# Asking for room in a ring of 24 once for six gathers

## What is computed

```python
h_self = x @ W_self.T + b_self
messages = x[src] @ W_neigh.T + b_neigh
h_neigh = jax.ops.segment_sum(messages, dst, num_segments=x.shape[0])
h = jax.nn.relu(h_self + h_neigh)
y = x + h
out = (y - mean(y)) / sqrt(var(y) + 1e-5)      # over the 128 features
```

## Time and profile before

| | before |
|---|---|
| median of three runs | 691.28 us (684.82 to 696.59) |
| the profiled execution | 693.77 us, span of its instructions 692.0 us |
| TensorE busy | 531.8 us (77%) |
| VectorE busy | 423.4 us (61%) |
| GpSimd busy | 405.3 us (59%), 391 gathers among it |
| ScalarE busy | 352.0 us (51%) |
| mean granted clock of TensorE | 0.88 of 2.4 GHz |

### The profile page before, as it was taken

How to read it: one execution, slowest core, us unless ns; L and a number is a source line. 1 busy time by engine, 2 the same in 40 slices (tenths; PEclk the granted TensorE clock), 3 DMA queues, 4 the chain that set the end, 5 groups by cost and what they waited for, 6 DMA issues and landing times.

```text
span 692.0 us, 12704 instructions
## 1 busy us (share of the span) xinstructions
PE 531.8 (77%) x3281; PEld 468.0 (68%) x3281; DVE 423.4 (61%) x1919; ACT 352.0 (51%) x1049; POOL 405.3 (59%) x424
## 2 busy tenths in 40 slices
PE   2046187878899769778877988888987897789895
PEld 0035076767778758667766867777877787678794
DVE  7883267688867657867747664644554535555564
ACT  1010055456555454655654655565655556456686
POOL 4777566666666645766557656656556656565400
PEclk9999589899798878988989989997789799888998
DMA  2422134444444454454443544444444434444443
GB/s 78 123 59 56 53 89 134 113 122 136 126 121 133 132 151 118 123 135 128 128 121 103 162 126 125 129 129 123 120 121 131 128 110 133 134 134 128 126 127 85
DMA packets 122942, 82.20 MB, mean 119 GB/s; under 512 B 15374, under 2 KB 115894, under 8 KB 122840
## 3 DMA queue, kind: packets, MB, share of 16 engines
q1 hardware_dynamic: 109208, 53.63, 27.5%
q0 software_dynamic: 13664, 27.77, 15.4%
HBM read 55.44 MB, written 26.71 MB: 119 GB/s over the span
## 4 chain that ended last, share of the span: by engine, by line
PE 61%; issue 15%; DVE 9%; another core or an unknown queue 6%; ACT 5%; DMA 2%; ACTq 1%; SPq 1%; POOL 0%; DVEq 0%
PE bank L889 17%; PE bank L912 16%; PE bank L913 13%; PE bank L877 6%; PE bank L908 5%; PE bank L894 3%; ACT result L1023 2%; DVE pick L730 2%; DVE y L740 2%; ACT sums_t L996 2%; DMA x_in<-in_x 1%; DVE below L530 1%; DMA end_dst<-in_dst 1%; ACT std L1013 1%
## 5 line engine op out<-in xcount | busy, mean ns | idle before, releaser
L482 POOL DMA_INDIRECT ring<-in_x,chunk_src x391 | 380.9, 974 | 236.3 <-issue 87.6
L996 ACT COPY sums_t<-bank 128x192 f32 x391 | 124.6, 319 | 290.5 <-remote 109.4
L889 PE MATMUL bank<-pick,ring 128*128 128x193 f32 (+1 forms) x782 | 188.8, 367 | 42.2 <-DVE pick L730 17.4
L912 PE MATMUL bank<-wsum_t,x_t 128*128 128x128 f32 (+1 forms) x782 | 188.3, 328 | 0.0
L913 PE MATMUL bank<-wn_t,sums_t 128*128 128x128 f32 (+1 forms) x782 | 174.5, 310 | 1.0 <-issue 0.9
L889 PEld LDWEIGHTS bank<-pick,ring 128*128 128x128 f32 x782 | 141.3, 215 | 49.5 <-issue 29.0
L1023 ACT ACTIVATE result<-y,minus_mean,rstd 128x128 f32<-128x128 f32 x391 | 163.5, 486 | 0.0
L912 PEld LDWEIGHTS bank<-wsum_t,x_t 128*128 128x128 f32 (+1 forms) x782 | 138.1, 221 | 26.8 <-issue 26.7
L740 DVE SCALAR_TENSOR_TENSOR y<-bank,x_in 128x384 f32<-128x384 f32 x131 | 72.6, 554 | 134.2 <-PE bank L913 65.2
L913 PEld LDWEIGHTS bank<-wn_t,sums_t 128*128 128x128 f32 (+1 forms) x782 | 141.1, 225 | 0.3 <-issue 0.2
L730 DVE TENSOR_SCALAR pick<-columns,local 128x194 f32<-128x194 f32 x391 | 106.3, 328 | 0.2
(11 more groups left out here) (118 smaller groups left out, 195.8 us busy)
## 6 DMA issues: line engine op xcount, KB each, us to landing
x_in<-in_x SPq DMA_DIRECT2D x130, 192.0 KB
out<-result SPq DMA_DIRECT2D x130, 192.0 KB
ring<-in_x,chunk_src POOLq DMA_INDIRECT x391
degrees_t<-degrees_dram SPq DMA_DIRECT2D x130, 2.2 KB
dst_padded<-in_dst SPq DMA_DIRECT2D x1, 390.6 KB
src_padded<-in_src SPq DMA_DIRECT2D x1, 390.6 KB
edge_src<-in_src SPq DMA_DIRECT2D x1, 390.6 KB
edge_dst<-in_dst SPq DMA_DIRECT2D x1, 390.6 KB
```

The lines of the kernel that those rows point to most:

```text
L482: nc.gpsimd.indirect_dma_start(ring[:, c % RING, :], None, x, bass.IndirectOffsetOnAxis(ap=chunk_src[:, c:c + 1], axis=0)).then_inc(gather ...
L889: ins = mm(into[:, frame:frame + SPAN + carried], ring[:, c % RING, :], pick[tau % DEEP][:, c % TRIO, 0:SPAN + carried], start=(c == 0), s ...
L912: mm(h, x_t[b][:, q, 0:rows], k.wsum_t[:], start=False, stop=False)
L996: nc.scalar.copy(sums_t[:, bass.ds(at, SPAN)], sum_bank[c // PAIR % SUM_BANKS][:, frame:frame + SPAN]).then_inc(sums_placed, 1)
```

## The change

GpSimd no longer asks for its place in the ring at every gather. At c = 24, 30, 36, ... it asks once for the six places of c to c + 5, that is, until chunk c + 5 - 24 is summed, and then issues six gathers. The last question, at c = 390, is the same as it was, since only one chunk is left. The question for the trio eight before stays. Everything else stays; all lines behind 76 move by one (L482 becomes L483).

```diff
 RING = 24
+BURST = 6
 GATHER_SEMS = 8
@@
                 if c % TRIO == 0 and tau >= GATHER_SEMS:
                     pool.wait_ge(gathered[tau % GATHER_SEMS], gathers_upto(tau - GATHER_SEMS))
-                if c >= RING:
-                    pool.wait_ge(chunks_summed, c - RING + 1)
+                if c >= RING and c % BURST == 0:
+                    pool.wait_ge(chunks_summed, min(c + BURST, CHUNKS) - RING)
                 nc.gpsimd.indirect_dma_start(ring[:, c % RING, :], None, x,
```

## The result

The changed kernel takes 723.66 us, the median of 5 runs (720.52 to 732.77); the kernel before, run beside it, 686.8 us (5 runs, 684.82 to 696.59). The ratio is 1.051, with an interval of 1.045 to 1.056: **about 5% slower**, where no change was forecast. The ratio leaves out executions in which the core was in a slower state, and the profiled one, the longest of the five with 732.77 us and a span of 731.0, is among these, so its rows overstate the loss by about 9 us.

The account below looks back on a forecast made before the run. TensorE's trios were taken to bound the kernel. Questions removed, the stricter question and other DMA work summed to 0 on TensorE's path: 693.8 us profiled again, median 691.3 us, range for 8 in 10 683 to 700.

Parts of the forecast that it names:

- A gather matters only where TensorE waits for its rows: TensorE's path: the kernel ends when TensorE's trios end; TensorE stood for a gather only three times, 7.8 us.
- the 62 forecast: GpSimd's waits for TensorE: to drop from 116 to about 62 and grow to 2 us or more each.
- a lead of 18 chunks: Ring of gathered rows: the stricter question lets GpSimd's lead over TensorE fall from 24 to 18 chunks.
- a landing well covered: Start of a burst: the first trio lands 5.4 us after it, against 20.3 us of TensorE work; least cover 14.9 us.
- an unchanged busy time: GpSimd: the same 391 gathers with a mean of 0.974 us, so busy time stays near 405 us.
- Cost taken: 0: Other work on the DMA engines: bursts delay no other transfers; at most 1.6 us for six gathers, cost 0.
- a sum over the DMA engines' time and x_in's lead: DMA engines: at most 0.27 us per gather, 1.6 us for six, against x_in loads issued 8.7 us ahead.
- The clock rival: TensorE's granted clock: mean 0.90 gives 677 us, 0.86 gives 705 us; chance 0.05 up, 0.03 down.
- the change gives or takes no wait of TensorE: TensorE: argument against the clock moving, beside three runs within 684.8 to 696.6 us without any change.
- The rival that nothing happens: GpSimd's gathers: bursts exist already, 116 waits for 367 gathers; ends at the forecast too, no chance of its own given.
- The Trainium skill's rule: Port pair: VectorE in a two-port mode and GpSimd take turns, the second stands; 12 us in all on GpSimd, sum 0.

Follow-up runs that it names:

- the first experiment: Kernel before, each gather still asking on its own but for the room of six (chunk c - 19 instead of c - 24): 692.66 us, ratio 1.001.
- those on the place: Changed kernel with its bursts moved: asks three chunks later 752.49 us; asks for two, four or five sums more 738.05, 737.07 and 734.87 us.

## Why the prediction was wrong

**The premise failed.** "A gather matters only where TensorE waits for its rows" is the step that sank it. TensorE waits for the rows as rarely as was said, three times and 7.8 us. But a gather also matters to engines that use none of its rows: while GpSimd issues gathers in a row, TensorE's results come late to ScalarE and VectorE, and TensorE then waits for those. All steps that counted GpSimd's own time and the ring's lead held: 59 waits for the 62 forecast, a lead of 18 chunks, a landing well covered, an unchanged busy time, no cost of the lower lead.

**"Cost taken: 0"** stood beside a sum over the DMA engines' time and x_in's lead. Both were right and both beside the point.

**The clock rival had the direction and part of the size, and was turned down on the premise.** It said that a clock of 0.86 makes 705 us. The runs of the changed kernel have 0.852 to 0.856, apart from the profiled one with 0.835, and 723.66 us: the clock fell as it said, but behind stops of TensorE, which it took for absent. Against it stood that "the change gives or takes no wait of TensorE"; it gives it the waits for ScalarE shown above.

**The rival that nothing happens** said that bursts exist already, in runs of 3.2, and so the change does little. But a run's cost is not in proportion to its length: asks for three (in runs of three and of six) cost 2%, for six 5%, for twelve 34%. The burst also removes a brake. With an ask at every gather, a late result stops GpSimd itself, and that stop ends the run. That this brake is what spares the kernel before is argued, from the first experiment and those on the place; no run shows it by itself.

**The Trainium skill's rule** on the port pair that VectorE and GpSimd share ("SBUF — State Buffer", Who interferes with whom) was the only way that the prediction weighed in which GpSimd's own work could hold up another engine. The traces agree that the port isn't it: ScalarE's copies have a mean of 319 ns with gathers and 318 with plain loads, VectorE's L740 has 556 in both. Neither is slower; what is late is when it starts.

**It was there to be read.** In the trace of before ScalarE stands 30.02 us for sums ended 21 us earlier, 109.4 us of its waits are put down to "remote" in a program on one core, and the chain has 6% of "another core or an unknown queue". I read that row of the chain and asked nothing of it.

## What to carry to other kernels

On a one-core kernel, look up every wait that the profile puts down to a remote or unknown releaser: compare when the work it waits for ended with when the waiter started, and see which engine was issuing what in between. Keep runs of transfers by index short, and let the engine that issues them stop where the others' results are late; a wait that seems to cost an idle engine nothing may be what lets the others' signals through. A deeper ring of gathers is not safer: 12 and 15 places beat 24 here, where the filling was one run of 33 gathers.

## What was not expected of the hardware

- While GpSimd issues transfers by index one after another (0.94 us each, 0.30 us apart), results of TensorE reach ScalarE and VectorE late: by 5.3 us in a run of 6, by 18.2 us in one of 27. With bursts of twelve VectorE starts on a trio's products 4.35 us after they end where that is within a run (median of 61), and 0.04 us where it is not (of 66). ScalarE's signals to SyncE are not late in a run (0.03 us). Iotas and plain loads by GpSimd, in runs as long as a burst, don't do this.
- In the burst shown above the trace also has the signals of TensorE themselves: those of seven pieces of work that ended from 438.42 to 442.25 are recorded between 443.59 and 443.98, in the order of the work. (Some records of other engines' signals are missing in that stretch.)
- Whether the matmul's own last columns are late or only its signal can't be told. By the Trainium skill ("Perfetto Trace Analysis", Tensor Engine Instruction (MATMUL, LD_WEIGHTS)) the end that a profile gives for a matmul is estimated, and its signal leaves only after the results are acknowledged. That fits a TensorE that seems to have ended work for which others still wait; no run here parts the two.
- Why TensorE's signals come late beside transfers by index, why the run of 27 let a result out 4 us before it ended, and why runs of six cost nothing with an ask at every gather stay open.
- After TensorE had stood, its granted clock was at 1.2 GHz for much of the next 10 us, in which a trio's products took 2.7 us in place of 1.4.
